# One matmul of 512 columns for two of 256 in the last expert stage, and a sum on VectorE behind it

## What is computed

```python
def _swiglu(u, w1, w2, w3):
    h = jnp.einsum('...d,hd->...h', u, w1)
    v = jnp.einsum('...d,hd->...h', u, w2)
    return jnp.einsum('...h,dh->...d', jax.nn.sigmoid(h) * h * v, w3)
...
_, top_idx = jax.lax.top_k(gate, K)          # K = 4 of E = 8 experts
...
eo = jnp.einsum('ebsh,edh->ebsd', jax.nn.sigmoid(h1) * h1 * h2, W3)
out = out + jnp.einsum('ebsd,bse->bsd', eo, weights)
```

## Time and profile before

| | us |
|---|---|
| median of three runs | 2012.91 |
| lowest and highest run | 2011.16, 2016.09 |
| the profiled execution | 2002.96 |
| its span | 2001.2 |
| TensorE busy in the span | 1553.0 |
| VectorE busy | 1270.7 |
| ScalarE busy | 778.5 |
| GpSimd busy | 787.2 |
| L1702, six matmuls in each chunk: busy, 1170 of them | 173.5 |
| L1778, the copy of a pack's output: busy, 39 of them | 26.3 |

### The profile page before, as it was taken

One profiled execution on the slowest core, in us unless ns is written; L12 is line 12 of the kernel. 1 busy time (PEld: TensorE's weight loads), 2 busy tenths in 40 slices (PEclk: granted clock), 3 DMA queues, 4 the chain that ended last, 5 costly groups with the idle time before them and its releaser, 6 DMA issues. The chain is left out here.

```text
span 2001.2 us, 38541 instructions
## 1 busy us (share of the span) xinstructions
PE 1553.0 (78%) x13148; PEld 1207.4 (60%) x13148; DVE 1270.7 (63%) x2435; ACT 778.5 (39%) x1652; POOL 787.2 (39%) x956
## 2 busy tenths in 40 slices
PE   5958577649998587781295889939996999999990
PEld 3536464527775254551053546517886999999990
DVE  4846457566665665558225777585674777777776
ACT  2311012315453143351032246622115777777770
POOL 1531112360001531002332350016885887878770
PEclk8969688869999788796697979968998999999995
DMA  2465543354312733309322443014116666666545
GB/s 94 161 172 165 144 124 105 118 172 122 101 43 75 192 78 74 76 8 345 119 69 78 145 122 96 28 40 146 60 65 227 211 237 212 235 208 239 207 153 210
DMA packets 286763, 274.00 MB, mean 137 GB/s; under 512 B 59033, under 2 KB 263676, under 8 KB 280958
## 3 DMA queue, kind: packets, MB, share of 16 engines
q1 hardware_dynamic: 260535, 229.35, 36.9%
q10 hardware_dynamic: 17376, 21.31, 3.4%
q0 software_dynamic: 8688, 21.16, 2.9%
HBM read 194.74 MB, written 79.35 MB: 137 GB/s over the span
## 5 line engine op out<-in xcount | busy, mean ns | idle before, releaser
L799 DVE TENSOR_REDUCE a_maxima<-psum 128x2 f32<-128x512 f32 x384 | 257.5, 687 | 151.5 <-PE psum L590 87.3
L770 ACT ACTIVATE a_probs<-psum 128x512 f32<-128x512 f32 x384 | 224.7, 598 | 260.3 <-PE psum L612 168.9
L97 PE MATMUL psum<-e_x_split,e_up_split 128*128 128x256 f32 x2340 | 311.7, 282 | 7.6 <-DVE e_x_split L1766 7.6
L97 PEld LDWEIGHTS psum<-e_x_split,e_up_split 128*128 128x128 f32 x2340 | 292.6, 189 | 8.0 <-DVE e_x_split L1766 8.0
L1810 POOL TENSOR_TENSOR e_up_split<-e_up_raw,e_up_split 128x512 fp32r<-128x512 f32 x195 | 252.7, 1297 | 88.9 <-ACT e_up_split L1732 87.1
L1702 PE MATMUL psum<-e_down_split,e_hidden_split 128*128 128x256 f32 x1170 | 173.5, 284 | 0.4 <-DVE e_hidden_split L1792 0.4
L1702 PEld LDWEIGHTS psum<-e_down_split,e_hidden_split 128*128 128x128 f32 x1170 | 152.5, 188 | 0.6 <-DVE e_hidden_split L1792 0.6
L590 PE MATMUL psum<-s_k_stack,s_q_stack 96*128 96x256 bf16 x512 | 121.2, 292 | 40.4 <-DMA a_rel_stack<-scr_r 28.7
L1787 DVE TENSOR_TENSOR psum<-psum,e_silu 128x256 f32<-128x256 f32 x195 | 83.7, 429 | 107.5 <-ACT e_silu L1753 107.4
L1771 DVE TENSOR_TENSOR e_down_split<-e_down_raw,e_down_split 128x256 fp32r<-128x256 f32 x195 | 145.8, 748 | 0.0
L1052 DVE TENSOR_TENSOR a_products<-psum,mask 128x512 f32<-128x512 f32 x128 | 82.7, 685 | 75.0 <-PE psum L985 74.9
(11 more groups left out here) (247 smaller groups left out, 3170.7 us busy)
## 6 DMA issues: line engine op xcount, KB each, us to landing
e_up_raw<-in_w_ffn SPq DMA_DIRECT2D x39, 1280.0 KB, 7.2
e_down_raw<-in_w_ffn SPq DMA_DIRECT2D x39, 640.0 KB, 4.2
scr_q<-p_parts SPq DMA_DIRECT2D x40, 384.0 KB, 2.7
scr_k<-p_parts SPq DMA_DIRECT2D x40, 384.0 KB, 2.8
a_q_stack<-scr_q SPq DMA_DIRECT2D x96, 128.0 KB, 3.0
s_q_stack<-scr_q SPq DMA_DIRECT2D x96, 128.0 KB, 2.6
s_k_stack<-scr_k SPq DMA_DIRECT2D x96, 128.0 KB, 2.7
a_k_stack<-scr_k SPq DMA_DIRECT2D x84, 128.0 KB, 3.0
```

The source lines that it names most:

```text
L97: last = eng.matmul(out, lhs(a, k), rhs(b, k), start=i == 0, stop=i == len(terms) - 1)
L770: act.activation(PB[:, u % PR], st_bank(u), ACT.Exp, scale=0.25).then_inc(S["probs"], 1)
L799: dve.tensor_reduce(MX[:, u // 8, :, u % 8], s_bank(u), AX.X, ALU.max).then_inc(S["s_used"], 1)
```

## The change

The two matmuls that have the high half of the gated product as their stationary operand become one, whose moving operand is both halves of the down weight side by side, 512 columns in two pieces of 256. Its result fills a whole PSUM bank: the first half of the bank holds high x high, the second high x low. The third matmul, low x high, is added to the second half. So the output of a pack now lies in two halves of each bank, and `take_out` has to add them: it copies the second halves to `e_y_pack`, waits for itself (`y_low`), and adds the first halves to it.

```diff
-        def down(r, a, m):
-            return SD[:, r, a, m * D:(m + 1) * D]
+        def down(r, m):
+            return SD[:, r, 0, m * D:(m + 1) * D]
+
+        def down_halves(r, m):
+            return SD[:, r, :, m * D:(m + 1) * D]
...
         def out_bank(i, t):
-            return ps[:, 4 + 2 * (i % 2) + t, 0:D]
+            return ps[:, 4 + 2 * (i % 2) + t, :]
...
                     for t in range(HALVES):
-                        for n, (a, b) in enumerate(((0, 0), (0, 1), (1, 0))):
-                            last = pe.matmul(out_bank(i, t), GS[:, a, c % 2, t * P:(t + 1) * P], down(i % 2, b, m),
-                                             start=m == 0 and n == 0, stop=m == n_h - 1 and n == 2)
+                        tokens = slice(t * P, (t + 1) * P)
+                        pe.matmul(out_bank(i, t), GS[:, 0, c % 2, tokens], down_halves(i % 2, m), start=m == 0, stop=m == n_h - 1)
+                        last = pe.matmul(out_bank(i, t)[:, D:2 * D], GS[:, 1, c % 2, tokens], down(i % 2, m),
+                                         start=False, stop=m == n_h - 1, skip_group_check=True)
                     last.then_inc(S["used"], 1)
...
-                    banks = ps[:, 4 + 2 * (i % 2):6 + 2 * (i % 2), 0:D]
-                    dve.tensor_copy(Y[:, i % 2], banks).then_inc(S["y_ready"], 1)
+                    banks = ps[:, 4 + 2 * (i % 2):6 + 2 * (i % 2), :]
+                    dve.tensor_copy(Y[:, i % 2], banks[:, :, D:2 * D]).then_inc(S["y_low"], 1)
+                    dve.wait_ge(S["y_low"], i + 1)
+                    dve.tensor_tensor(Y[:, i % 2], banks[:, :, 0:D], Y[:, i % 2], ALU.add).then_inc(S["y_ready"], 1)
```

More of the change, by code:

```diff
@@ L1600, in streamed @@
         names = ["x_turned", "x_hi", "x_lo", "up_hi", "up_lo", "down_hi", "down_lo", "up_done", "silu", "hidden", "g_hi",
-                 "g_lo", "used", "y_ready", "id_ready", "added", "stored"]
+                 "g_lo", "used", "y_low", "y_ready", "id_ready", "added", "stored"]
         S = {n: ph.sem(n) for n in names}
```

## The result

The changed kernel takes 2062.15 us (median of six runs, 2059.54 to 2068.84); the kernel before took 2011.31 in six runs of the same comparison. The ratio is 1.0258, interval 1.0236 to 1.0280. The prediction was 2010.6 us with a range of 2006 to 2017, within 0.3% of the kernel before. It was wrong: the change costs 2.6%.

What follows compares the result with a forecast made beforehand. TensorE was taken as the bound; matmuls -3.9, the last sum on the path +0.7 and TensorE waits +0.9 gave -2.3 us, from 2012.91 to 2010.6 us, range 2006 to 2017.

Steps and rivals of the forecast that it cites:

- Part 1: TensorE's matmuls: one of 512 columns replacing two of 256 saves 10 ns, 390 times, 3.9 us (3.5 to 4.7).
- Part 2: VectorE's added sum in take_out: about 0.68 us per pack, hidden beside TensorE except the last, +0.7 us.
- Part 3: Whether VectorE's 0.70 us delay per pack is hidden: TensorE waits about 0.1 us once in four packs, +0.9 us.
- the loop: VectorE's delay returns through ScalarE and GpSimd to L1771, growing about 0.33 us a round, resetting at the fourth.
- GpSimd's remaining lag: GpSimd's 0.70 us delay less the 0.41 us wait it meets: 0.29 us, passed to the next pack's L1771.
- the bound of 9.9 us: Upper bound on TensorE's waits: 0.29 us in each of 34 packs from the fifth on, without a reset.
- Rival (a): VectorE and GpSimd hold TensorE up in every pack: +6.7 us, 2019.6 us, slower; chance 0.13.
- the slack of 1.74 us: Time between L1787, VectorE's gated product of chunk 3, and TensorE's make_hidden needing it; 0.70 goes, 1.04 us remain.
- (b): A 512-column matmul costs what two of 256 do, saving nothing: about 2013.8 us, within 0.3%; chance 0.12.
- (c): Matmul turn-over goes altogether, 512 columns take 216 ns, saving 8.6 us: 2005.0 to 2005.9 us, faster; chance 0.05.

Runs made afterwards that it cites:

- the last experiment: Changed kernel with VectorE's low half of the down weight (L1775) moved behind the low half of the gated product (L1798) in each chunk: 1.0220, 2051.26 us.

## Why the prediction was wrong

**Part 1, the matmuls: right.** 10 ns forecast with 9 to 12 as bounds, 12 measured where nothing else holds TensorE; 390 x 12 ns = 4.7 us, the upper end. That TensorE's gain is the program's as long as the others keep up was right too, and the condition failed.

**Part 2, the sum: right in size.** 0.69 us, not held itself (690 to 693 ns), 0.7 on the path at the end.

**Part 3, the hiding: this step failed.** It put the loss at 0.9 us; measured are some 55 (51 in all, and 4.7 gained less 0.7 for the tail). It named the place and the chain, from the sum over L1793, ScalarE and GpSimd's L1810 back to L1771; that chain is the one in the timelines, and it goes when GpSimd no longer reads or when L1793 is no longer pushed. Two sentences in it were wrong.
- "VectorE's instruction is first, isn't held, and the loop starts anew." I took the recorded start for the moment at which an instruction gets its operands' path. VectorE's comes first by 0.10 to 0.15 us in the changed kernel and is held 73 times out of 73. What I took for the exit of the loop is its steady state.
- The price of a hold. I let L1771 be late by GpSimd's remaining lag, 0.29 us a round, because in the kernel before it is held for the rest of one GpSimd instruction. Held from its own start it loses all of one (1.73 us), and all of two where GpSimd, being late, has two in a row (2.95).

From the second followed the bound of 9.9 us. Rival (a), which had the mechanism and the side, had that price too and forecast 2019.6 us; it was given 0.13, because GpSimd and ScalarE have a quarter of their time idle, and it was tied to the slack of 1.74 us. Both were read rightly, but they are not what decides. What decides is whether a rhythm changes, and a push of 0.29 us was enough for it in five packs. I also followed L1771 of two chunks alone, and not that of the other three, where in the changed kernel both long holds lie (at 1775.53 and 1778.05, the next pack's first two chunks).

**Rivals (b) and (c)** are out: a pack of 11.02 us is a distance of 12 ns less, neither none nor 22.

## What to carry to other kernels

Where two engines hold each other up, the slack of a single chunk doesn't say what a delay costs: walk the timeline until it closes, with all instructions of both engines, and ask whether the delayed pattern repeats by itself. Work added to an engine that is not the bound belongs where that engine waits; here the same instruction cost over 50 us in one place and nothing that the packs show one chunk later. And a push in one pack alone is a cheap experiment that tells a cost from a change of rhythm.

## What the runs showed of the hardware

**The start in the record is not when VectorE gets in.** Over the changed kernel and the experiments with long holds, of L1771 (L1775) that started with no L1810 running and saw one start soon after, all that were ahead by 0.148 us or less were held until it was over (464 of 464, the changed kernel's 73 among them); all that were ahead by 0.170 us or more ran through in 0.42 us (81 of 81, all in the last experiment, where another instruction stands ahead of it). A part of the lead is no lead: by its record L1775 starts some 0.09 us before the instruction ahead of it on VectorE ends (1778.05 against 1777.70 + 0.43 = 1778.13 in the changed kernel). The Trainium skill, "SBUF — State Buffer", section "SBUF: two separate sides", says that of such two instructions the one that starts first has the shared path for its whole length and the other is blocked. By the recorded starts the trace agrees only beyond some 0.15 us of VectorE's lead.

**No turn between two of the same engine.** VectorE, waiting, was not let in between two GpSimd instructions that followed each other without a gap (2.54 us for two, hold of 2.95; 36 times in the changed kernel).

What stays open is how the kernel before gets into its good rhythm in the first packs each time, and whether a change that moves these engines by another 0.3 us, anywhere in the stage, would tip it. In all its runs here it stayed within 2000.8 and 2017.7 us. What makes up the 12.39 us of a pack in the last experiment stays open too.
